# A mamba block with a mixture of experts in fp32: two of eight drive products on TensorE, residual and norm sums on TensorE and ScalarE, prologue and router in another order

## The reference, cut to what matters

```python
x = x + attn(_layernorm(x))          # a mamba block
x = x + ffn(_layernorm(x))           # 8 experts, 2 per row

def attn(x, ...):
    h = _layernorm(x) * ln_g + ln_b
    x_in, z = split(h @ W_in)                         # 512 channels each
    u = silu(causal_conv4(x_in) + conv_b)
    dt, Bm, Cm = split(u @ W_xproj)                   # 64, 16 and 16 columns
    delta = softplus(dt @ W_dt + b_dt)
    s_t = exp(delta_t * A) * s_{t-1} + (delta_t * u_t) * B_t    # 16 states a channel
    y_t = sum_n s_t[n] * C_t[n]
    return x + ((y + u * D) * silu(z)) @ W_out

def ffn(x, ...):
    logits = x @ Wg + bg                              # top 2 of 8, softmax weights
    y = sum of two experts' relu(x @ W1 + b1) @ W2 + b2, weighted, plus x
    return layernorm(y) * gamma + beta
```

## Time and profile before

| | before |
|---|---|
| median of three runs | 2542.03 us |
| the profiled execution, its own time | 2553.05 us |
| its span, first to last instruction | 2551.3 us |
| PE, DVE, ACT, POOL busy in the span | 81%, 83%, 55%, 77% |
| mean granted TensorE clock | 0.900 |
| first scan, last scan ended, first tile of the experts' matmuls | 74.2, 1885.2, 1959.5 us |

### The profile page before, as it was taken

One profiled execution on the slowest core, in us unless ns is written; L12 is line 12 of the kernel. 1 busy time (PEld: TensorE's weight loads), 2 busy tenths in 40 slices (PEclk: granted clock), 3 DMA queues, 4 the chain that ended last, 5 costly groups with the idle time before them and its releaser, 6 DMA issues. The chain is left out here.

```text
span 2551.3 us, 41205 instructions
## 1 busy us (share of the span) xinstructions
PE 2055.1 (81%) x11191; PEld 1561.7 (61%) x11192; DVE 2123.9 (83%) x3249; ACT 1408.2 (55%) x2909; POOL 1965.7 (77%) x1233
## 2 busy tenths in 40 slices
PE   6769687796968787796968787796754999999988
PEld 2446465564646555565646555564653999999973
DVE  1899999999999999999999999999962556555657
ACT  4666766767676766766675776766431222222216
POOL 1899899999999999999999999999962222222227
PEclk9889898898989798898989898898765999999999
DMA  3240413224040413214041413314034777777769
GB/s 102 87 150 10 141 57 126 85 91 157 18 167 33 151 51 124 102 74 166 21 155 35 149 60 116 113 55 166 11 120 139 223 227 230 227 227 231 227 197 332
DMA packets 177827, 328.42 MB, mean 129 GB/s; under 512 B 19539, under 2 KB 100979, under 8 KB 177556
## 3 DMA queue, kind: packets, MB, share of 16 engines
q1 hardware_dynamic: 147172, 274.00, 33.6%
q0 software_dynamic: 12624, 34.62, 3.6%
q10 hardware_dynamic: 17888, 18.11, 2.1%
HBM read 272.25 MB, written 54.41 MB: 128 GB/s over the span
## 5 line engine op out<-in xcount | busy, mean ns | idle before, releaser
L729 POOL TENSOR_TENSOR dbu<-du,bb 128x1024 f32<-128x1024 f32 x512 | 1199.0, 2355 | 13.4 <-DVE ps_a L564 9.0
L960 ACT ACTIVATE ps_a<-dl,a_neg 128x512 f32<-128x512 f32 x1024 | 683.0, 683 | 151.4 <-DVE wd L577 75.5
L1162 PEld LDWEIGHTS ps_y<-ident,wd 128*128 128x128 f32 x2816 | 376.5, 158 | 112.9 <-issue 82.9
L1162 PE MATMUL ps_y<-ident,wd 128*128 128x128 f32 x2816 | 425.6, 299 | 16.5 <-DVE wd L577 16.5
L564 DVE TENSOR_TENSOR_SCAN ps_a<-ps_a,carry,dbu 128x512 f32<-128x512 f32 x352 | 437.5, 1276 | 0.1
L1440 POOL DMA_INDIRECT eo_scratch<-ow,idx x135 | 129.9, 962 | 391.3 <-DVE ow L1394 385.4
L577 DVE TENSOR_TENSOR wd<-ps_a,rows_c 128x1024 f32<-128x1024 f32 (+1 forms) x384 | 426.9, 1112 | 0.0
L564 DVE TENSOR_TENSOR_SCAN ps_a<-ps_a,dbu 128x512 f32<-128x512 f32 x352 | 417.1, 1216 | 4.1 <-ACT ps_a L960 3.7
L746 POOL TENSOR_TENSOR wp<-ss,rows_c 128x1024 f32<-128x1024 f32 (+1 forms) x192 | 382.0, 1990 | 15.2 <-DVE ss L564 7.5
L1549 PE MATMUL e_ps_h<-xT,w 128*128 128x128 f32 x2160 | 264.9, 276 | 0.0
L1380 DVE TENSOR_SCALAR e_hT<-e_ps_h,b_turned 128x128 f32<-128x128 f32 x540 | 152.1, 344 | 134.7 <-PE e_ps_h L1549 133.7
(11 more groups left out here) (166 smaller groups left out, 2798.5 us busy)
## 6 DMA issues: line engine op xcount, KB each, us to landing
w<-in_L_ffn_W_dram SPq DMA_DIRECT2D x135, 512.0 KB
bb<-b_scratch SPq DMA_DIRECT2D x128, 512.0 KB, 4.3
rows_c<-b_scratch SPq DMA_DIRECT2D x128, 512.0 KB, 6.6
xt<-xs_scratch SPq DMA_DIRECT2D x135, 129.0 KB
ee<-eo_scratch SPq DMA_DIRECT2D x64, 256.0 KB, 7.2
xb<-in_L_attn_x_dram SPq DMA_DIRECT2D x16, 512.0 KB, 3.7
hx<-in_L_attn_x_dram SPq DMA_DIRECT2D x16, 512.0 KB, 5.4
x_scratch<-hx SPq DMA_DIRECT2D x16, 512.0 KB, 3.3
```

The costliest lines, as they stand in the source:

```text
L729: pool.tensor_tensor(dbu[:, k % NBU], du[:, g % 2, :].unsqueeze(1).broadcast_to([P, 2, CH]), bb[:, 2 * m:2 * m + 2, :], ALU.mult).then_inc ...
L960: act.activation(ps_a[:, bank(k), :], dl[:, g, :], ACT.Exp, scale=a_neg[:, g, n:n + 1]).then_inc(exp_done, 1)
L1162: ins = pe.matmul(ps_y[:, i, :], wd[:, s % NWD, h, i * P:(i + 1) * P], ident[:], start=False, stop=False, is_transpose=True, skip_group_ch ...
```

## The change

- Of the eight drive products of a group, those of states 4, 5 and 10, 11 (`BMS = (2, 5)`) are no longer made by GpSimd. TensorE turns `du` (`turnu`, 4 transposes a group), ScalarE copies it to `duT`, and the drive is a matmul of `duT` with diagonal matrices that hold B (`drive`, 4 states x 4 matmuls of 128 x 128 a group) into the PSUM bank in which the scan also leaves its states. The exp of these states goes to the free `dbu` buffer. The diagonals are made once a chunk by ScalarE, 16 activations over 128 x 128, from B turned by TensorE (`bturn`). Two of eight B row loads go.
- State 15 becomes held: GpSimd's third product with C is as wide as the others (12 and 15), and VectorE's single product for state 15 goes. A group has five direct pairs, whose banks alternate from group to group. `TURN_P` and `WEIGH_P` are later by one or two steps.
- The residual is added by TensorE, with a matmul of `ident` with `hx` at the end of each output product. ScalarE empties the result with two activations that also give the row sums. The squares for the router's norm are four more activations with a sum. VectorE's L592, L487 and L494 go.
- The router runs a chunk earlier (38 to 46 steps after the start of chunk q+1). `STEADY` and all other tables have new places.
- Ahead of the loop, W_in comes in two halves, five small loads go through ScalarE's queue with semaphores of their own, TensorE no longer waits for all weights, and only dt of groups 0 and 1 is made there. The z projections, dt of 2 and 3 and silu(z) of chunk 0 move into its steps (`START`, `SILU_Z = 70`).
- `tile_table` and `aside` lie in the memory of `hT`.

```diff
+    BMS = (2, 5)
+    NTP = len(BMS)
-    DIRECT = (1, 4, 7, 10, 13, 15)
+    DIRECT = (1, 4, 7, 10, 13)
...
-        NW = 13
+        NW = 8
-                 ("conv", 3), ("dbc", 0), ("dt", 0), ("dt", 1), ("z", 0), ("dt", 2), ("z", 1), ("dt", 3), ("z", 2),
-                 ("z", 3)]
+                 ("conv", 3), ("dbc", 0), ("bturn", 0), ("dt", 0), ("dt", 1), ("turnu", 0)]
+        START = [("z", 0, 0, 0, 1, 1), ("z", 1, 0, 0, 1, 2), ("z", 2, 0, 1, 1, 3), ("z", 3, 0, 2, 1, 4),
+                 ("h", 0, 1, 4, 1, 2), ("h", 1, 1, 5, 1, 2), ("x", 0, 1, 8, 1, 2), ("x", 1, 1, 10, 1, 2),
+                 ("turnu", 1, 0, 13, 1, 2)]
+        STEADY = [("h", 0, 1, 0, 1, 3), ("h", 1, 1, 1, 1, 5), ("x", 0, 1, 4, 2, 3), ("back", 3, -1, 6, 1, 2),
+                  ("dt", 2, 0, 9, 1, 2), ("out", 0, -1, 10, 1, 4), ("turnu", 1, 0, 10, 1, 5),
+                  ("out", 1, -1, 14, 2, 4), ("x", 1, 1, 17, 1, 5), ("conv", 0, 1, 18, 2, 2), ("conv", 1, 1, 21, 2, 5),
+                  ("x", 2, 1, 24, 2, 3), ("x", 3, 1, 25, 1, 4), ("dt", 3, 0, 29, 1, 2), ("conv", 2, 1, 27, 3, 5),
+                  ("turnu", 2, 0, 33, 1, 4), ("conv", 3, 1, 30, 4, 8), ("turnx", 0, -1, 37, 1, 4),
+                  ("turnx", 1, -1, 37, 1, 4), ("logit", 0, -1, 40, 1, 0), ("dbc", 0, 1, 41, 1, 4),
+                  ("back", 0, 0, 42, 1, 3), ("bturn", 0, 1, 43, 1, 3), ("rank", 0, -1, 43, 1, 1),
+                  ("back", 1, 0, 45, 1, 3), ("turnu", 3, 0, 47, 1, 1), ("dt", 0, 1, 48, 1, 1), ("dt", 1, 1, 49, 1, 2),
+                  ("z", 0, 1, 53, 2, 2), ("z", 1, 1, 54, 2, 4), ("z", 2, 1, 56, 2, 5), ("turnu", 0, 1, 59, 1, 2),
+                  ("z", 3, 1, 59, 2, 4), ("back", 2, 0, 60, 1, 4)]
+        XL_AT = 12
+        SILU_U = 41
+        SILU_Z = 70
+        ADD_DT = ((50, 0), (51, 1), (75, 2), (96, 3))
+        STATS_X1 = (27, 27)
+        XN = (35, 38)
+        ROUTE = (38, 38, 38, 39, 39, 39, 39, 39, 39, 42, 45, 46, 46, 46)
+        SCATTER = ((25, 0, 0), (26, 0, 1), (26, 0, 2), (27, 0, 3), (28, 1, 0), (29, 1, 1), (30, 1, 2), (33, 1, 3))
+        DIAGONALS = (53, 59, 64, 64)
+        DRIVE = (4, 5, 10, 10)
+        TURN_D = {9: 0, 10: 1, 14: 2, 17: 3, 20: 4}
+        TURN_P = {10: 0, 19: 1, 20: 2}
+        SKIP_Y = 7
+        WEIGH_P = {4: 0, 7: 1, 9: 2}
...
         def held(n):
-            return n % 3 == 0 and n < N - 1
+            return n % 3 == 0
...
             def scan(c, g, n):
-                if n % 2 == 0:
-                    dve.wait_ge(dbu_done, k // 2 + 1)
+                if n // 2 in BMS:
+                    dve.wait_ge(tb_done, driven(t, n))
+                elif n % 2 == 0:
+                    dve.wait_ge(dbu_done, products(t, n // 2))
...
-                if n == 0 and 0 < t <= LAST + 1:
-                    weigh(t - 1, 5)
...
-                if t <= LAST:
+                if t <= LAST and m not in BMS:
                     times_b(t, m)
...
+            def stats_x1(q, step):
+                if step == 0:
+                    for j in range(2):
+                        act.wait_ge(*emptied("out", j, q))
+                    if q > 0:
+                        act.wait_ge(prm1, q)
+                    act.mul(nm[:, 1, :], sums[:], -1.0 / D).then_inc(lnr_step, 1)
+                else:
+                    act.wait_ge(lnr_step, 2 * q + 1)
+                    if q > 0:
+                        act.wait_ge(scat, 16 * 2 * NT * q)
+                        act.wait_ge(proj_full, full("turnx", 1, q - 1))
+                    for i in range(NT):
+                        ins = act.activation(stage[:, i, 0:D], hx[:, i, :], ACT.Square, bias=nm[:, 1, i:i + 1],
+                                             accum_out=sqs[:, i:i + 1])
+                    ins.then_inc(lnr_step, 1)
...
+                elif kind == "turnu":
+                    act.wait_ge(tb_done, 2 * NTP * (q * G + g))
+                    act.copy(duT[:].rearrange("p i d -> p (i d)"), src).then_inc(taken, 1)
...
+                elif kind == "out":
+                    for i in range(2 * g, 2 * g + 2):
+                        ins = act.activation(hx[:, i, :], src[:, (i - 2 * g) * D:(i - 2 * g + 1) * D], ACT.Copy,
+                                             accum_out=sums[:, i:i + 1])
...
+            def diagonals(q, j):
+                p = j // 2
+                act.wait_ge(*emptied("bturn", 0, q))
+                if q > 0:
+                    act.wait_ge(tb_done, 2 * (NTP * (G * q - 1) + p) + 2)
+                for i in range(2 * (j % 2), 2 * (j % 2) + 2):
+                    for h in range(2):
+                        ins = act.activation(dg[:, p, h, i, :], ident[:], ACT.Copy, scale=bT[:, i, p, h:h + 1])
...
+                dst = ps_a[:, bank(k), :]
                 j = before(k)
-                if j is not None:
+                if n // 2 in BMS:
+                    dst = dbu[:, k // 2 % NBU, n % 2, :]
+                    if k // 2 >= NBU:
+                        act.wait_ge(scan_done, k - n % 2 - 2 * NBU + 2)
+                elif j is not None:
...
-                                        wout[:, k, :], start=(k == 0), stop=(k == G - 1))
+                                        wout[:, k, :], start=(k == 0), stop=False)
+                        if k == G - 1:
+                            pe.wait_ge(xl_done, q + 1)
+                            ins = pe.matmul(dst[:, i * D:(i + 1) * D], ident[:], hx[:, 2 * g + i, :], start=False,
+                                            stop=True)
...
+            def drive(t, p, h):
+                c, g = t // G, t % G
+                k = t * N + 2 * BMS[p] + h
+                if h == 0:
+                    pe.wait_ge(*emptied("turnu", g, c))
+                    pe.wait_ge(dg_done, NTP * c + p + 1)
+                    for j in (before(k), before(k + 1)):
+                        if j is not None:
+                            pe.wait_ge(*released(j))
+                            if j // SG % 2 == 0:
+                                pe.wait_ge(carry_act, kept(j))
+                for i in range(NT):
+                    ins = pe.matmul(ps_a[:, bank(k), i * P:(i + 1) * P], duT[:, i, :], dg[:, p, h, i, :], start=True,
+                                    stop=True)
+                ins.then_inc(tb_done, 1)
...
-            pe.wait_ge(w_in, 16 * NW)
-            pe.wait_ge(zeroed, 26)
+            pe.wait_ge(zeroed, 25)
```

More of the change, by code:

```diff
@@ L273, in due, with there @@
             c, rest = divmod(at - offset, span)
[L274 removed]
+            return c + d if rest == 0 and 0 <= c + d < NC else None
+        uses = sorted([(*u, True) for u in START] + [(*u, False) for u in STEADY], key=lambda u: u[3] + u[4])
+        def there(kind, g, d, c, once):
+            return c == 0 if once else c > 0 or (kind, g, d) not in [u[:3] for u in START]
         table = [(kind, g, 0, -1, 1, 0) for kind, g in FIRST]
         for c in range(NC + 2):
[L278 to L279 removed]
+            table += [(kind, g, c + d, c * SG + at, parts, lag) for kind, g, d, at, parts, lag, once in uses
+                      if 0 <= c + d < NC and there(kind, g, d, c, once)]
         for u, v in zip(table[len(FIRST):], table[len(FIRST) + 1:]):
@@ L304, in bank @@
             n = k % N
-            return NA - 1 if held(n) else 2 * (product(n) % 2) + n - DIRECT[product(n)]
+            return NA - 1 if held(n) else 2 * ((ND * (k // N) + product(n)) % 2) + n - DIRECT[product(n)]
         def states(k, wide):
@@ L722, in times_b @@
                 k = t * HB + m
+                row = 2 * brow(m)
                 if g == 0:
@@ L1156, in turn_d @@
             def turn_d(t, j):
-                s = 6 * t + j
+                s = ND * t + j
                 pe.wait_ge(wd_done, s + 1)
-                for h in range(2 if j < 5 else 1):
+                for h in range(2):
                     for i in range(NT):
@@ L1183, in turns @@
                 if t <= LAST:
+                    for j in range(2 * NTP):
+                        if n == DRIVE[j]:
+                            drive(t, j // 2, j % 2)
                     if n == SKIP_Y:
@@ L1199, in _ @@
                 turns(at // N, at % N)
-                for kind, g, d, offset, parts, _ in STEADY:
+                for kind, g, d, offset, parts, _, once in uses:
                     for part in range(parts):
                         q = due(at, offset + part, d)
-                        if q is not None:
+                        if q is not None and there(kind, g, d, q - d, once):
                             project(kind, g, q, part, parts)
```

317 lines of the change are left out of this document (169 added, 148 removed), and 3 rows, old and new, of the table STEADY.

## The result

| | before | after |
|---|---|---|
| median on one chip, five runs each | 2542.79 us (2540.58 to 2546.16) | 2529.98 us (2528.30 to 2531.37) |
| ratio, 95% interval | | 0.9939 (0.9925 to 0.9952) |
| span of the profiled execution | 2551.3 us | 2527.5 us |
| prologue, main loop, hand-over, experts | 74.2, 1811.0, 74.3, 591.8 us | 52.1, 1824.7, 58.9, 591.8 us |
| VectorE idle in the main loop | 68.0 us | 148.4 us |

The change makes the kernel 12.8 us faster, not 100. Both ends gave more than forecast; the main loop, which should have lost 72 us, became 13.7 us longer. No run shows in which stage those 10 us lie, so that the loop may have grown by more.

What follows compares the result with a forecast made beforehand. VectorE (96% busy) and GpSimd (97%) were taken to bound the main loop together. Main loop 72, prologue 16 and hand-over 12 us less make 100, so 2542 - 100 = 2442 us, range 2382 to 2512.

Steps and rivals of the forecast that it cites:

- With VectorE's idle time kept at 68 us: Main loop: VectorE's idle time stays as before, so 82 us less work gives 1811 - 82 = 1729 us.
- I take TensorE as just not binding: Main loop: TensorE, 106.2 us busy of 108 a chunk, nearly full but not the bound, since long waits get shorter.
- The step from the profiled execution to the median: Whole kernel: profiled execution would be 2453 us; it stands 11 us above the median, so the forecast is 2442.
- Rival A: Main loop: TensorE becomes the bound; 2473 us at 96% busy, 2512 with its present losses; chance 0.24.
- Rival C: Every group: drives come late behind the turn of GpSimd's last product; 2570 us at 2.0 us a group; chance 0.10.
- VectorE: Main loop: state 15's product, residual and norm statistics leave VectorE, 82.0 us less in sum.
- The swapped form of the scan at zero: Four in sixteen scans, drive in PSUM and exp in SBUF: no change in time, 13 us allowed either way.
- The wait for state 15 (10 us): Group starts: exp of state 0 must wait for scan 15; 0 to 38 us over 64 groups, taken as 10.
- Prologue: Before the loop: first scan at 56.5 us, a gain of 17.7, 2 given back for silu(z), net 16.
- Hand-over: Last scan to first expert tile: chunk 14's router and its scatters leave the path, net 12 us less.
- GpSimd: Main loop: two drive products go, third product with C widens; falls by 231 us to 1528, no bound on the mean.
- would mean A or C: Sign in the main loop: long waits of a scan for TensorE's drive, states 4 and 10, point to those rivals.

Runs made afterwards that it cites:

- e6: Kernel after, with four of a chunk's eight GpSimd scatters moved into the next chunk's first group and `row_meta` from 55 to 62; 2504.78 us.
- e15: e13 with the drives made as one-pass turns by the identity (B left out for states 4, 5, 10, 11); 2442.54 us.
- e12: e6 with the drives made as one-pass turns by the identity (B left out for states 4, 5, 10, 11); 2480.97 us.
- e7: Kernel after, with the output product made over the first of four channel blocks only; 2530.11 us.
- e9: e6 with the output product made over the first of four channel blocks only; 2489.58 us.
- e13: e9 with ScalarE emptying the second output product's bank two of its steps earlier, ahead of group 1's exps of states 0 and 1; 2457.49 us.
- e14: e6 with ScalarE emptying the second output product's bank two of its steps earlier, nothing left out; 2507.08 us.

## Why the prediction was wrong

It gave 2442 us with a range of 2382 to 2512; measured was 2529.98, a gain of 0.6% where "faster" had 0.90.

- **The step that failed: "With VectorE's idle time kept at 68 us", and behind it "I take TensorE as just not binding".** The idle time went to 148.4 us, where the sum had 68 and 10 for the exp of state 0: 70 of the 86 us between 1739 and 1824.7, the other 15 being VectorE's own work. The busy row was sized well (106.2 us a chunk forecast, 1661.12 / 16 = 103.8 measured), but TensorE, busy 91% in a fixed order, had no room here to absorb a late input. e6 wins 29 us by moving scatters out of a chunk's last group, which had made GpSimd late at the next chunk's start; e15 wins another 60 by taking TensorE's work away and moving ScalarE's exit. As e15 leaves work out, the 60 us say what that limit costs, not what a complete kernel can win.
- **The step from the profiled execution to the median.** The forecast took 100 us off the profiled execution (2453) and another 11 because that one stood above the median. The kernel after has no such surplus (2529.27 against 2529.98). Of the 88 us by which the median missed, 76 are the stages (86 in the loop, less 6 and 3 at the ends), 12 this step.
- **What a share of busy time told.** In the kernel after TensorE's matmul is busy 1661.12 of 1824.68 us (91%), its weight load 1274.54 (70%). The 70% were no sign that its work cost nothing: e6, where the weight load is busy 1269.55 of 1795.6 us (71%), won 21.8 us when e12 took 97 us of matmul time away (1652.24 to 1555.11). Nor are the 91% a threshold: the same 5.3 us a chunk were worth 0 (e7), 0.9 (e9) and, with the exit, 2.9 us (e13 against e14).
- **Rival A** (TensorE binding, losses as before, 2512; with the loop at 1811 its own sum gives 2514) was the nearest: 18 us off. It had the engine, not its mechanism.
- **Rival C** named the mechanism of group 0 (the turn of GpSimd's last product ahead of the drives, at half clock, 0.50 in chunk 9), but for all groups; the trace shows it at the start of a chunk above all (TensorE waits 50.3 us for that product in group 0, 9.9 in group 3), since the scatters of the group before delay GpSimd there (e6). It priced a GpSimd that is one product late and gave it little weight, because GpSimd "has room". It has, on the mean.
- **VectorE.** Forecast 82.0 us less, measured 66.7. Counted on the timeline from each start to the next, the removed instructions took 79 us inside the loop; the last chunk's share of the 82 lay in the hand-over. Against them stand 7 us more of the router's small steps (15 chunks' in the loop, 14 before, and 2.0 us a chunk in place of 1.6), and 2 to 3 us more each of the gate, the products and the scans. The working had none of these. The swapped form of the scan at zero was right: 1218 ns where the common one takes 1211, and 1276 against 1270 with a carry.
- **The wait for state 15 (10 us)** was looked for at the wrong reader. VectorE's scans of state 0 hardly wait, 5.8 us in all. ScalarE does, 95.6 us in all for scans into `ss` (56.6 before), and what is behind it in its queue, the exit of the output product, carries the delay to TensorE and from there to the gate as soon as TensorE has less to do there (e7, e9, against e13).
- **Prologue.** First scan at 52.1 us, forecast 56.5. But more than 2 us were given back: four waits for exps and softplus in chunk 0's group 0 sum to 13.8 us:

```profile
56.66 1.23 DVE L587 TENSOR_TENSOR_SCAN ps_a<-ps_a,dbu 128x512 f32<-128x512 f32 x1 [3.31 <-ACT ps_a L1017]
60.45 1.23 DVE L587 TENSOR_TENSOR_SCAN ps_a<-ps_a,dbu 128x512 f32<-128x512 f32 x1 [2.55 <-ACT ps_a L1017]
...
70.34 1.22 DVE L587 TENSOR_TENSOR_SCAN ss<-ps_a,dbu 128x512 f32<-128x512 f32 x1 [3.60 <-ACT ps_a L1017]
83.80 0.69 DVE L559 SCALAR_TENSOR_TENSOR dl<-ps_p,dl 128x512 f32<-128x512 f32 x1 [4.29 <-ACT dl L988]
```

  What left the prologue (z, silu(z), dt of groups 2 and 3, diagonals) is ScalarE's work that VectorE now waits for with the loop running. The gross gain was 22.1 us, the net one some 8.
- **Hand-over** 15.4 us less, forecast 12; **experts** 591.8 as forecast; **GpSimd** 1554.8 us, forecast 1528; TensorE's mean granted **clock** in the loop rose from 0.88 to 0.95, as forecast without a size.
- **The signs were named.** Long waits of scans for TensorE's drive "would mean A or C": 49.0 us, and both are part of it. The forecast was to be wrong "if the loop is above 1765": 1824.7.

## What to carry to other kernels

When a change takes the slack of one engine to give another its time back, keep the idle time of before in no sum (here it went from 68.0 to 148.4 us): list what every wait of each queue has behind it. Here the wait for the scan of state 15 reached the gate through ScalarE, whose late exit held TensorE for 25.0 us in e9. A mean load says nothing of the moment; GpSimd, busy 85%, kept TensorE standing 3.4 us once a chunk (50.3 us in 15), and moving four scatters was worth more than the whole change had been. And if removing work at a wait gives nothing, lift the next suspect together with it before clearing either: in group 1 one edit alone gave 13.7 us and the other nothing, both together 43.0.
